# Another mapping of matrix rows to partitions for three weight loads of a fused LoRA and FFN kernel

## What is computed

```python
base = x @ W.T                                   # W: 512 x 512
logits = x @ Wr.T + 5.0 * one_hot(language, 8)   # Wr: 8 x 512
gates = softmax over the two largest logits, 0 elsewhere
h = einsum('btd,erd->bter', x, A)                # A: 8 x 16 x 512
lora = einsum('bter,bte,eor->bto', h, gates, B)  # B: 8 x 512 x 16
c = base + 2.0 * lora
out = x + (c @ sign) * softplus(scale)           # sign: 512 x 512
```

## Time and profile before

| | |
|---|---|
| median of 3 runs | 168.5 us (168.42 to 169.45) |
| profiled execution | 168.52 us |
| its span, first to last instruction | 166.7 us |
| TensorE (PE) busy | 160.5 us, 96% of the span |
| VectorE (DVE) busy | 96.0 us, 58% |
| ScalarE (ACT) busy | 65.7 us, 39% |
| GpSimd (POOL) busy | 53.5 us, 32% |
| granted TensorE clock | full in every slice |
| HBM read, written | 11.03 MB, 8.39 MB |

### The profile page before, as it was taken

The page is one execution under the profiler, slowest core; times in us unless marked ns, Lnnn a source line. Parts: engine busy times, 40 slices in busy tenths (PEclk is TensorE's granted clock), DMA queues, the critical chain, the costliest instruction groups (busy, mean ns, idle before and its releaser), DMA issues.

```text
span 166.7 us, 3732 instructions
## 1 busy us (share of the span) xinstructions
PE 160.5 (96%) x1082; PEld 154.4 (93%) x1082; DVE 96.0 (58%) x416; ACT 65.7 (39%) x176; POOL 53.5 (32%) x51
## 2 busy tenths in 40 slices
PE   7799998999999999999999999999999999999993
PEld 5588777999999999999999999999999999999982
DVE  5358969655555555555555555555555555555451
ACT  3355453433333444444434443444333333444240
POOL 2683876033333333333333222222333333333000
PEclk9999999999999999999999999999999999999999
DMA  4998214233333333333333333333333333111113
GB/s 125 290 225 160 85 37 124 65 120 119 123 124 121 126 126 126 126 126 126 123 110 100 113 118 117 120 119 120 117 118 124 113 127 122 63 67 63 63 65 126
DMA packets 26311, 19.51 MB, mean 117 GB/s; under 512 B 4128, under 2 KB 21312, under 8 KB 26304
## 3 DMA queue, kind: packets, MB, share of 16 engines
q1 hardware_dynamic: 25728, 18.38, 36.4%
q10 hardware_dynamic: 576, 1.05, 1.8%
HBM read 11.03 MB, written 8.39 MB: 116 GB/s over the span
## 4 chain that ended last, share of the span: by engine, by line
PE 86%; DVE 6%; DMA 3%; ACT 2%; issue 1%; DVEq 0%
PE pair L625 64%; PE pair L642 13%; DMA w_in<-in_L_cond_W 3%; PE p_ht L649 2%; PE pair L580 2%; PE pair L594 2%; PE pair L587 2%; DVE xt L435 1%; DVE second L533 1%; DVE wide_lo L486 1%; DVE m_full L482 1%; ACT wide_hi L374 1%; DVE top_no L528 1%; PE pair L562 1%; PE pair L561 1%
## 5 line engine op out<-in xcount | busy, mean ns | idle before, releaser
L305 POOL TENSOR_TENSOR xt_lo<-xt,xt_hi 128x512 fp32r<-128x512 f32 x32 | 41.1, 1287 | 90.0 <-ACT xt_hi L356 89.9
L625 PE MATMUL pair<-wide_hi,xt_hi 128*128 128x256 f32 (+2 forms) x260 | 63.2, 320 | 0.3 <-POOL xt_lo L305 0.2
L625 PE MATMUL pair<-wide_hi,xt_lo 128*128 128x256 f32 (+2 forms) x260 | 60.3, 310 | 0.0
L625 PE MATMUL pair<-wide_lo,xt_hi 128*128 128x256 f32 (+2 forms) x260 | 60.3, 309 | 0.0
L625 PEld LDWEIGHTS pair<-wide_hi,xt_hi 128*128 128x128 f32 x260 | 40.1, 189 | 1.5 <-POOL wide_lo L321 0.6
L625 PEld LDWEIGHTS pair<-wide_hi,xt_lo 128*128 128x128 f32 x260 | 40.3, 188 | 0.0
L625 PEld LDWEIGHTS pair<-wide_lo,xt_hi 128*128 128x128 f32 x260 | 40.2, 188 | 0.0
L400 ACT ACTIVATE y<-pair 128x256 f32<-128x256 f32 x31 | 11.9, 385 | 45.0 <-PE pair L642 45.0
L510 DVE TENSOR_TENSOR logits<-pair,bias 128x8 f32<-128x8 f32 x32 | 5.3, 164 | 35.9 <-PE pair L625 35.9
L435 DVE STREAM_TRANSPOSE xt<-x_in 128x512 f32<-128x512 f32 x32 | 22.7, 710 | 3.7 <-DVE top L518 3.2
L356 ACT ACTIVATE xt_hi<-xt 128x512 fp32r<-128x512 f32 x32 | 20.3, 634 | 2.6 <-DVE xt L435 2.6
(11 more groups left out here) (76 smaller groups left out, 133.5 us busy)
## 6 DMA issues: line engine op xcount, KB each, us to landing
x_in<-in_x SPq DMA_DIRECT2D x128, 64.0 KB, 1.9
out<-y SPq DMA_DIRECT2D x31, 256.0 KB, 2.1
sign_in<-in_L_ffn_sign ACTq DMA_DIRECT2D x4, 256.0 KB, 7.3
w_in<-in_L_cond_W SPq DMA_DIRECT2D x4, 256.0 KB, 6.8
a_in<-in_L_cond_A SPq DMA_DIRECT2D x4, 64.0 KB, 6.6
b_in<-in_L_cond_B SPq DMA_DIRECT2D x1, 256.0 KB, 7.5
out<-y SPq DMA_DIRECT2D x2, 128.0 KB, 1.8
wr_in<-in_L_cond_Wr SPq DMA_DIRECT2D x4, 4.0 KB
```

The source lines that it names most:

```text
L305: nc.gpsimd.tensor_tensor(xt_lo[n][:, :, :].rearrange("p j (g b) -> p g j b", g=NQ), xt[n][:, :, :, :], xt_hi[n][:, :, :].bitcast(FP32).re ...
L625: last = nc.tensor.matmul(pair[n][bank][:, at0:at0 + hi - lo], l[:, k, :], w[:, k, lo:hi], start=(opens and k == 0 and l is xt_hi[n] and w ...
```

## The change

Rows of W and sign go to partitions in two halves: part j = 2h + i holds, in partition p, the row 256h + 2p + i. Each load still has 128 runs of 2 KB. Where the runs of one load lay 8 KB apart over the whole matrix, they now lie 4 KB apart in one half of it; parts 0 and 1 cover the first half, parts 2 and 3 the second. B must follow, and in that mapping a partition's rows for one expert are two pairs instead of four in a row: B is loaded by two transfers of 1024 runs of 128 bytes each, on the same semaphore, and the wait for it goes from 16 to 32. In SBUF each B element lands where it did before.

```diff
-    w_load = W.rearrange("(p j) d -> p j d", j=OC)
-    sign_load = sign.rearrange("(p j) n -> p j n", j=OC)
+    w_load = W.rearrange("(h p j) d -> p h j d", h=2, p=P)
+    sign_load = sign.rearrange("(h p j) n -> p h j n", h=2, p=P)
...
-    b_load = B.rearrange("e (p j) r -> p e (j r)", j=OC)
+    b_load = B.rearrange("e (h p j) r -> h p e (j r)", h=2, p=P)
...
-        b_in = sb("b_in", [P, E, OC * R])
+        b_in = sb("b_in", [P, E, 2, OC * R // 2])
...
-                sp_eng.dma_start(w_in[:, j, :], w_load[:, j, :]).then_inc(w_loaded[j], 16)
+                sp_eng.dma_start(w_in[:, j, :], w_load[:, j // 2, j % 2, :]).then_inc(w_loaded[j], 16)
...
-            sp_eng.dma_start(b_in[:, :, :], b_load).then_inc(b_loaded, 16)
+            for h in range(2):
+                sp_eng.dma_start(b_in[:, :, h, :], b_load[h, :, :, :]).then_inc(b_loaded, 16)
...
-                act.dma_start(sign_in[:, j, :], sign_load[:, j, :]).then_inc(sign_loaded[j], 16)
+                act.dma_start(sign_in[:, j, :], sign_load[:, j // 2, j % 2, :]).then_inc(sign_loaded[j], 16)
...
-            act.wait_ge(b_loaded, 16)
-            nc.scalar.activation(b_hi[:, :, :, :], b_in[:, :, :].rearrange("p e (j r) -> p j e r", j=OC),
+            act.wait_ge(b_loaded, 32)
+            nc.scalar.activation(b_hi[:, :, :, :], b_in[:, :, :, :].rearrange("p e h (j r) -> p (h j) e r", h=2, r=R),
                                  ACT.Copy).then_inc(b_hi_made, 1)
...
-            nc.vector.tensor_tensor(b_lo[:, :, :, :], b_in[:, :, :].rearrange("p e (j r) -> p j e r", j=OC),
+            nc.vector.tensor_tensor(b_lo[:, :, :, :], b_in[:, :, :, :].rearrange("p e h (j r) -> p (h j) e r", h=2, r=R),
                                     b_hi[:, :, :, :].bitcast(FP32), ALU.subtract).then_inc(b_lo_made, 1)
```

## The result

The changed kernel takes 167.22 us (median of 4 runs, 166.91 to 167.48), the kernel before 168.82 on the same chip (4 runs, 168.42 to 169.45). The ratio is 0.989 with a 95% interval of 0.985 to 0.993, so it is faster by some 1.1%, where I had forecast it 0.4% slower. The profiled execution took 166.99 us for 168.52, its span is 165.2 us for 166.7. The difference of 1.5 us is all in the first 28 us.

The account below looks back on a forecast made before the run. TensorE, busy from 29.4 to 160 us, was taken as the bound, so only the start could move. The profiled 168.52 us plus 0.7 for B, all other terms 0, gave 169.2 us, range 167.8 to 170.3.

Parts of the forecast that it names:

- What bounds the kernel: TensorE is busy from 29.4 to 160 us, so only shifts in the start count, and they reach the end unchanged.
- W and sign at a 4 KB pitch: Early loads of W and sign: same packets, bytes and order, so the HBM rate was taken as unchanged, 0 us.
- Its own upper bound, 1.4 us: Early loads of W and sign: at best 0.63 MB go at 408 GB/s, moving all later landings up 1.4 us.
- a gain of over 1%: Whole kernel below 166.8 us, needing the first rival's whole gain and no price for B; chance 3%.
- B in 128-byte runs: B's load: twice the packets land it 0.8 us later, of which ScalarE hides 0.1, costing 0.7 us.
- The straight line: B's load: packet price extended from 2 KB and 256 bytes to 128 bytes, 14.6 to 19.0 ns each.
- if only bytes count, 0: B's load: lower bound of its delay, 0 us, if doubling the packets costs nothing.
- The first rival: Early loads: the pitch held the rate, so W and sign land sooner; 167.8 us, up to 168.5; chance 17%.
- at most the 1.00 us gap: TensorE's start: with W landing earlier, M's sum gains no more than the 1.00 us idle from 4.9 to 5.9.
- SP's extra issue at 0: SP's queue: one more DMA issue of 0.45 us disappears in the stand against the full queue; cost 0.
- the prediction's estimate: B's load: by the skill page's beat counts, 128-byte packets take 1.64 times as long, 0.76 us later.

Follow-up runs that it names:

- e6: Kernel before with the queues swapped, sign on SP's queue and W on ScalarE's, mapping as before: 169.07 us, ratio 1.006.
- e2: Kernel before with only B's load changed, to two transfers of 128-byte runs in the new mapping: 168.67 us, ratio 1.000.
- e3: Kernel before with the halves mapping on W alone: 168.21 us, ratio 0.996.
- e4: Kernel before with the halves mapping on sign alone: 168.21 us, ratio 0.996.
- e5: Kernel before with W and sign mapped in quarters (part j holds row 128j + p), B loaded as before: 167.39 us, ratio 0.992.
- e1: Changed kernel with B loaded as before, in one transfer of 256-byte runs in the old mapping: 167.34 us, ratio 0.992.
- d3: Kernel before with W and sign in quarters and B's load issued ahead of those of x and A: 167.50 us, ratio 0.990.
- c1: Changed kernel with GpSimd's xt_lo of tile 0 moved ahead of its wait for the language numbers: 167.00 us, ratio 0.990.
- c2: Kernel before with GpSimd's xt_lo of tile 0 moved ahead of its wait for the language numbers: 168.08 us, ratio 0.997.

## Why the prediction was wrong

- What bounds the kernel: right. TensorE practically without a gap once the steps run, and a shift at VectorE's chain (1.56 us at scale, 1.55 at m_full) that reaches the end as 1.5. All 18 profiles end about 150.8 us after m_full's start.
- The step that failed is "W and sign at a 4 KB pitch ... I take 0". Its own upper bound, 1.4 us, was near the truth: 1.56 measured at scale's landing. The reason given for 0 was that W's packets took 170 ns and sign's 77 at the same pitch. e6 shows that this difference is the queue's: with the matrices swapped, sign's take 150. So a low price on one queue didn't clear the address pattern; why SP's queue had the high one was not tried. The row that spoke was the sum of both: 210 GB/s against 408 for equal packets. I gave this case 17%, and 3% to a gain of over 1%.
- B in 128-byte runs: the term of 0.7 us was mis-sized. The straight line gave 14.6 to 19.0 ns; 13.9 were measured in the change, and e2, B's split alone, cost 0.0 us (ratio 0.997 to 1.003), with B landing 0.5 us earlier in its profile. The bound "if only bytes count, 0" was the right value, and the second transfer's stand at the full queue did no harm.
- The first rival had the right mechanism and lost it in the sum: 168.52 - 1.4 = 167.1 is the profiled time to a tenth (166.99), but I added B's 0.7 to it. The 1.4 itself was partly luck: it supposed 408 GB/s from 2.5 to 5.5 us, and 319 came, worth 3.0 - 0.63 / 0.319 = 1.0 us; the rest came after that window, and from 5 to 7 us the changed kernel has 311 and 391 GB/s for 203 and 330. With B's price at zero nothing was to be added. Adding the whole 0.7 wasn't sound even with that price, because the same faster queue brings B forward and can give it slack. How much differs from profile to profile. Between the end of b_hi and that of A's transpose lie 0.97 us in the changed kernel (13.67 and 14.64). With B in one transfer they are 0.40 in e3, 0.59 in e4 and 1.10 in e5, and none in e1.
- TensorE's gain "at most the 1.00 us gap": M's sum began 1.26 us earlier (the warm-up ended at 4.65), but this didn't decide; VectorE did.
- SP's extra issue at 0: right in its effect. The language numbers landed 1.2 us earlier like all else, and xt_lo (16.52) stayed clear of VectorE.
- The Trainium skill's page DMA: Bandwidth & Descriptors would, by the prediction's estimate, have had B 0.76 us later (sections "Why small descriptors are slow (HBM only)" and "How a descriptor splits into AXI transactions"). The runs don't bear it out: the byte rate with 128-byte packets, 155 GB/s, was 7% below the 167 of the earlier trace rows, not 1.64 times lower.

## What to carry to other kernels

When a load's runs are shorter than their pitch and all lie at one place modulo that pitch, compare the rate with that of another stretch with the same packet size; a factor of two is a reason to spread them, and which rows go to which partition is free wherever the index is summed away. Where two parts of a change share a queue, don't just add their terms; try each alone and both together. What brings a load forward can give slack to those behind it: B landed at 15.50 before, at 15.02 with its split alone, at 14.46 with the mapping alone, and at about 12.95 with both. A cost that lands on one queue's packets isn't proof about the addresses until the queues have been swapped. And look for one instruction whose start tells the end, as m_full's does here: it says at once which other shifts can matter.

## What the runs showed of the hardware

- The rate of 2 KB reads from two 1 MB matrices depended on where the runs of a load lay. From 2.5 to 5.5 us it was 191 to 213 GB/s with all runs of a load in one 2 KB slot of the 8 KB blocks, 319 to 368 with two slots, and 327 to 393 with four; with four slots over the whole matrices it was 393 and 402 from 3 to 5 us, for 219 and 166. Loads that read one slot's rows again and again had 297, which the slots don't explain.
- 128-byte packets went at 13.9 ns each over 16 engines, 155 GB/s, hardly below the byte rate of 256-byte ones.
- Two loads of 128 four-byte packets from GpSimd's queue went along with 103 GB/s in a microsecond that had 311 without them (one profile each); not tried by themselves.
- VectorE's subtractions took longer beside GpSimd's: 1.15 for 0.19 us, 1.37 for 0.65, 1.46 for 0.72, 1.52 for 0.65, each beside a GpSimd subtraction. In e2 and d3 the VectorE piece ended only after the GpSimd one had (18.31 after 18.26, 16.10 after 15.55). A transpose on VectorE took its usual 0.70 us beside one (c1, at 13.96). Which of the two starts first hangs on a landing, which would fit that the runs of the kernel before fall into groups (none of the eleven beside c2 between 168.25 and 169.07).
- With loads to 32 partitions issued right behind W, W's third part landed at 8.40 us, and at 6.65 with B's load to 128 partitions put between (one profile each).
